# Ternary feed-forward layer: the scaling of the 1408-wide hidden row moves from VectorE to ScalarE

## The reference

```python
def activation_quant(x):
    scale = 127.0 / jnp.clip(jnp.max(jnp.abs(x), axis=-1, keepdims=True), 1e-05, None)
    return jnp.clip(jnp.round(x * scale), -128, 127) / scale

def weight_quant(w):                       # weights of -1, 0, 1
    scale = 1.0 / jnp.clip(jnp.mean(jnp.abs(w)), 1e-05, None)
    return jnp.clip(jnp.round(w * scale), -1, 1) / scale

def bitlinear(x, w):
    return jnp.einsum('bsh,oh->bso', activation_quant(x), weight_quant(w))
...
x = rmsnorm(x, weight)
gate, up = split(bitlinear(x, w_gate_up))  # 512 -> 2 x 1408
hidden = square(relu(gate)) * up
return bitlinear(hidden, w_down)           # 1408 -> 512
```

## Time and profile before

| | |
|---|---|
| median of three runs | 1764.09 us (1761.99, 1764.09, 1770.47) |
| the profiled execution, its own time | 1760.03 us |
| its span, first to last instruction | 1758.3 us |
| busy: PE, DVE, ACT, POOL | 1363.1, 1424.3, 936.0, 545.6 us |
| mean granted TensorE clock | 0.892 of full speed |
| phase L0f | from 224 to 401 us of the span; its matmuls from 233 us |
| L1101, the operation that the change moves | 16 times, 15.3 us in all, 953 ns each |
| L1030, GpSimd's rounding that follows it | 16 times, 45.2 us in all, 2825 ns each |

### The profile page before, as it was taken

The page is one execution under the profiler, slowest core; times in us unless marked ns, Lnnn a source line. Parts: engine busy times, 40 slices in busy tenths (PEclk is TensorE's granted clock), DMA queues, the critical chain, the costliest instruction groups (busy, mean ns, idle before and its releaser), DMA issues. The chain is left out here.

```text
span 1758.3 us, 23962 instructions
## 1 busy us (share of the span) xinstructions
PE 1363.1 (78%) x6614; PEld 1011.7 (58%) x6614; DVE 1424.3 (81%) x3156; ACT 936.0 (53%) x1936; POOL 545.6 (31%) x569
## 2 busy tenths in 40 slices
PE   4889358886999667266771992489999899998888
PEld 2444224444788443254620882368888788876776
DVE  5999769985887468799488799888999889878785
ACT  3477646652333362466425441358888788733443
POOL 0000014442110022200013122214777577766541
PEclk8899779998999757688885996799999999999999
DMA  6230020000000210355200100416889799887974
GB/s 213 90 123 13 0 78 1 0 0 1 1 1 1 86 61 1 93 194 179 68 1 0 48 25 1 125 49 208 248 245 251 210 263 256 251 235 234 261 231 157
DMA packets 92286, 197.93 MB, mean 113 GB/s; under 512 B 16040, under 2 KB 25384, under 8 KB 91312
## 3 DMA queue, kind: packets, MB, share of 16 engines
q0 software_dynamic: 27120, 91.25, 18.9%
q1 hardware_dynamic: 65088, 105.82, 18.3%
HBM read 181.30 MB, written 15.73 MB: 112 GB/s over the span
## 5 line engine op out<-in xcount | busy, mean ns | idle before, releaser
L2379 POOL DMA_INDIRECT L3f_gd<-rows,idx x160 | 188.4, 1178 | 202.2 <-DVE L3f_gd L2608 177.0
L2379 POOL DMA_INDIRECT L3f_gu<-in_L_ffn_e_up,idx x160 | 168.4, 1052 | 71.2 <-issue 47.2
L2447 PE MATMUL L3f_o_ps<-L3f_euh,L3f_ath 128*128 128x512 f32 x352 | 146.4, 416 | 22.4 <-DVE L3f_atl L2589 19.5
L2435 PE MATMUL L3f_h_ps<-L3f_xh,L3f_edh 128*128 128x512 f32 (+1 forms) x384 | 144.0, 375 | 6.7 <-DVE L3f_xl L2594 6.7
L2419 PE MATMUL L3f_g_ps<-L3f_oh 128*128 128x128 f32 x704 | 97.0, 282 | 61.5 <-DVE L3f_oh L2576 61.5
L2435 PE MATMUL L3f_h_ps<-L3f_xh,L3f_edl 128*128 128x512 f32 (+1 forms) x384 | 144.0, 375 | 0.0
L2435 PE MATMUL L3f_h_ps<-L3f_xl,L3f_edh 128*128 128x512 f32 (+1 forms) x384 | 143.9, 375 | 0.0
L1030 POOL TENSOR_TENSOR wgu<-L0f_hid,magic 128x1408 bf16<-128x1408 f32 x16 | 45.2, 2825 | 315.2 <-DVE L0f_hid L1101 315.2
L2447 PE MATMUL L3f_o_ps<-L3f_eul,L3f_ath 128*128 128x512 f32 x352 | 138.9, 395 | 0.0
L2447 PE MATMUL L3f_o_ps<-L3f_euh,L3f_atl 128*128 128x512 f32 x352 | 138.9, 395 | 0.0
L2419 PEld LDWEIGHTS L3f_g_ps<-L3f_oh 128*128 128x128 f32 x704 | 90.9, 194 | 72.0 <-issue 67.4
(11 more groups left out here) (555 smaller groups left out, 3729.3 us busy)
## 6 DMA issues: line engine op xcount, KB each, us to landing
L3f_eu<-in_L_ffn_e_up SPq DMA_DIRECT2D x96, 256.0 KB
L3f_ed<-in_L_ffn_e_down SPq DMA_DIRECT2D x96, 256.0 KB
L2x_ed<-in_L_ffn_e_down SPq DMA_DIRECT2D x32, 256.0 KB, 3.3
rows<-L2x_eo SPq DMA_DIRECT2D x32, 256.0 KB, 2.4
wgu<-in_L_ffn_w_gate_upT SPq DMA_DIRECT2D x4, 1408.0 KB, 7.5
X<-in_x SPq DMA_DIRECT2D x4, 1024.0 KB, 10.2
L0x_V<-in_ctxT SPq DMA_DIRECT2D x8, 512.0 KB, 3.9
L1f_C<-in_ctx SPq DMA_DIRECT2D x2, 2048.0 KB, 12.9
```

The source lines that it names most:

```text
L2379: pool.indirect_dma_start(buf[j % ND][:, :], None, table, bass.IndirectOffsetOnAxis(ap=idx[:, j:j + 1], axis=0)).then_inc(sem[j % ND], 16)
L2435: last = pe.matmul(h_ps[h][:, 0:cols], lhsT=w[h][:, c, :], rhs=x[:, c, 0:cols], start=(c == 0 and m == 0), stop=(c == DC - 1 and m == 2))
L2447: last = pe.matmul(o_ps[a][:, :], lhsT=w[h][:, a * P:(a + 1) * P], rhs=x[h][:, :], start=False, stop=False)
```

## The change

The scaling of the hidden row becomes a ScalarE operation (Identity with scale and bias, where the bias is a column that holds MAGIC). It is issued at the head of ScalarE's turn n for tile n+1, with a wait for that tile's scale; for tile 0 it is issued ahead of the turns, after the first chunk of tile 1. VectorE's L1101 and its wait are removed. GpSimd waits on the same semaphore as before, which ScalarE now raises.

```diff
     @block.scalar
...
-        count_from_two(act, xq_ready, xqT_ready, rl_ready, sq_ready, hqT_ready)
+        count_from_two(act, xq_ready, xqT_ready, rl_ready, sq_ready, hqT_ready, hk_ready)
...
+        def scale_hidden(n, h):
+            act.wait_ge(hs_ready, n + 3)
+            act.activation(hid[h][:, :], hid[h][:, :], ACT.Identity, scale=s[:, bass.ds(n, 1), 6], bias=magic[:, 0:1]).then_inc(hk_ready, 1)
+
         def one(n, h):
+            if within(n, 1):
+                scale_hidden(n + 1, 1 - h)
             hidden_turned(n, h)
...
         for j in range(NCH):
             up(1, 1, j)
+            if j == 0:
+                scale_hidden(0, 0)
         steps(act, one)
...
     @block.vector
...
             dve.tensor_scalar(at(s, n, 6), at(s, n, 6), 127.0, at(s, n, 4), ALU.mult, ALU.mult).then_inc(hs_ready, 1)
-            dve.wait_ge(hs_ready, n + 3)
-            dve.tensor_scalar(hid[h][:, :], hid[h][:, :], at(s, n, 6), MAGIC, ALU.mult, ALU.add).then_inc(hk_ready, 1)
```

More of the change, by code:

```diff
@@ L1038, in _ @@
     def _(dve):
-        count_from_two(dve, xn_ready, am_ready, ac_ready, ar_ready, as_ready, xm_ready, hid_ready, hm_ready, hc_ready, hr_ready, hs_ready, hk_ready, x_ready, st_ready)
+        count_from_two(dve, xn_ready, am_ready, ac_ready, ar_ready, as_ready, xm_ready, hid_ready, hm_ready, hc_ready, hr_ready, hs_ready, x_ready, st_ready)
         n = row_stats(dve, stats, m[:, :], var[:, :], w1[:, :], w2[:, :], step, 0)
```

## The result

| | before | changed |
|---|---|---|
| median of the runs | 1763.04 us (1755.72 to 1770.47, 4 runs) | 1791.09 us (1788.48 to 1794.19, 4 runs) |
| ratio, 95% interval | | 1.0158 (1.0123 to 1.0192) |
| span of the profiled execution | 1758.3 us | 1786.8 us |
| VectorE busy, ScalarE busy | 1424.3, 936.0 us | 1413.2, 955.9 us |
| phase L0f, its first VectorE operation (L100) to the next phase's (L129) | 177.3 us | 205.0 us |

The change costs 28 us, 1.6%. VectorE has 11 us less to do and the kernel is slower by 28: all of it lies in the phase L0f (27.7 us). What comes before the phase ended 1.8 us later in this execution and what comes after it took 1.0 us less, which makes the 28.5 of the spans.

A forecast was written before the change was run, and what follows sets the result against it. VectorE was taken to set the pace in L0f. Ring 25.2, start 0.3, end 1.2 and clock 3.3 make 30.0 us on the profiled 1760.03, so 1790; the median, 3 higher, is 1793 us, range 1782 to 1803.

The forecast's parts named there:

- The ring: L0f loop: chain from scale through scaling, copies, ReLU, square to first product takes 4.2 us, not 2.40; 25.2 us in all.
- hand-over: Signal from VectorE's scale operation to ScalarE's scaling, taken as 0.15 us within the 4.2, bounded by 0.03 and 0.16.
- VectorE's cover: Removing L1101 saves VectorE 0.95 us a turn; alone a turn could gain only 0.41, and here it returns as waiting.
- not slower: Rival: the scaling fits into ScalarE's wait at the turn's head; gain 5.7 us, giving 1757; chance 0.04.
- The start: Tile 0's scaling between the first and second chunk of tile 1 delays products: +0.3 us, between 0 and 0.9.
- The end: Tile 14's down projection waits for copies behind tile 15's scaling: +1.2 us, between 0 and 1.3.
- The clock: TensorE's longer idle before the third chunk halves its clock: 0.7 us in a third of the turns, 3.3 us.
- GpSimd: Its rounding gets its tile about 0.8 us later but has a whole turn of slack; costs nothing.

The follow-up runs named there:

- e5: The changed kernel with 24 extra 128x128 transposes on TensorE ahead of the third chunk; ratio 1.0142 to the kernel before, stage 202.9 us.
- e1: The kernel before with only the wait for the scale put at the head of ScalarE's turn, scaling still on VectorE; ratio 1.0021 to the kernel before.
- e2: The changed kernel with the scaling issued behind ScalarE's two copies of the hidden row instead of ahead; ratio 1.0060 to the kernel before.
- e6: The changed kernel with one more 128x512 f32 ScalarE operation between the wait for the scale and the scaling; ratio 1.0221 to the kernel before.
- e4: The kernel before without any scaling of the hidden row, GpSimd waiting for the scale instead; ratio 1.0025, loop turns 9.31 and 11.22 us.
- e11: The changed kernel run again unaltered; ratio 1.0143 to the kernel before, stage 205.2 us.
- e8: The changed kernel with scaling behind the first chunk's square, split: 704 columns on ScalarE, 704 on VectorE; ratio 1.0129 to the kernel before.
- e3: The changed kernel with the scaling issued behind the first chunk's square; ratio 1.0000 to the kernel before, loop turn 9.67 us.
- e7: The kernel before without scaling of the hidden row, GpSimd's rounding also waiting for VectorE's L1065 of that turn; ratio 0.9961 to the kernel before.
- e9: e8 with GpSimd's rounding also waiting for VectorE's scaling of a token row (L1089); ratio 0.9970 to the kernel before.

## Why the prediction was right

The forecast was 1793 us, 30 us of cost; measured 1791.09, 28 us of cost.

- **The ring (1.8 us a turn, 25.2 in all).** Measured 4.20 us from the scale to the product, forecast 4.2; 7.37 for the rest, forecast 7.3. The 14 turns grew by 26.1 us with the clock's falls and by 25.1 in e5, without them. The hand-over that I bounded by 0.03 and 0.16 was 0.17 (0.04 in e1's turn above, with the copy behind the wait), the scaling 1.56 (forecast 1.55). e1, e2 and e6 move the term as the ring says: the wait alone 0.3 a turn, behind the copies 0.85, with 0.72 us of work more about 0.7 more.
- **VectorE's cover.** I gave the removal of L1101 no gain in the sum, and none is there. Its worth by itself, forecast 0.41 a turn, was 0.38 in e4's short turns. The rival "not slower" fell with L1107's place: ScalarE's wait for it is 46.6 us.
- **The start (+0.3)** did not show: the part until tile 1 took 30.1 us against 30.6.
- **The end (+1.2)** was 2.0. The down projection starts 3.16 us after the start of the last scale's operation instead of 2.00, so the 1.2 itself is right, but the projection then ran longer than before: 4.22 us before, now 4.88 from 419.79 to 424.67. The part after the turns has 6.8 us at the low clock, 3.4 before and in e5, where it took 13.7 us, 0.9 above before.

```profile
416.63 0.21 DVE L1107 TENSOR_SCALAR L0f_s<-L0f_s 128x1 f32<-128x1 f32 x1
419.79 1.89 PE L949 MATMUL L0f_o_ps<-wgu,L0f_hqT 128*128 128x512 bf16 x4 [4.15 <-ACT L0f_hqT L999]
421.90 2.77 PE L949 MATMUL L0f_o_ps<-wgu,L0f_hqT 128*128 128x512 bf16 x6 [0.22 <-issue]
```

- **The clock (3.3 us)** is the mis-sized term. I had a third of the turns hit; six of 14 have a stretch at 0.50. But they cost 1.1 us in all and not 0.7 each: against e5's turns one cost 0.76, two 0.2 and 0.1, three nothing. I took 0.7 from the one turn in which the clock was low from the first matmul of the third chunk; the kernel before has that turn too, so that some of the 1.1 is no growth. In the turn shown above TensorE resumes at full clock (307.79, 0.82 us) and falls only afterwards, by these stretches of the changed kernel:

```profile
308.00:310.00 2.00, 1.48 (x9) 0.59 (x8) 1.96 (x6) 0.96 (x3) 0.88 (x1) 0.74 0.00 0
310.00:312.00 2.00, 2.00 (x8) 0.98 (x9) 1.83 (x4) 1.30 (x3) 0.00 (x0) 0.50 0.00 0
```

The third product is then 3.89 us after the first, hardly late (3.82 before), and what is slow is the down projection, which has slack: that turn is 11.57 us, as the others. The falls in the turns of the changed kernel, e11 and e6 line up by the distance from the first product to the fall, which I had left out (14th turn, which has less work, not counted; by the clock granted in the trace):

| the clock falls, us after the first product | the third product is late by |
|---|---|
| 0.1 to 0.8 (5 falls) | 0.7 to 0.8 |
| 0.9 (3) | 0.55 to 0.57 |
| 1.1 to 1.2 (3) | 0.34 to 0.37 |
| 1.3 and 1.4 (2) | 0.18, 0.11 |
| 1.5 and more (6) | nothing |

So 0.7 is what a fall costs that comes with the third chunk's first matmul, and most come later. Why a fall comes where it does in a turn stays open.

- **GpSimd** I costed at nothing, and that is nearly so by the order of this change and not by slack, as e4 and e8 show. Its rounding starts at 304.73, after VectorE's front operation is over. Its last weight operation meets VectorE's scaling of a token row (L1087 here), which takes 0.66 us in the loop and up to 0.82 instead of 0.49:

```profile
307.88 1.00 POOL L1042 TENSOR_TENSOR Wl<-Wr,Wh  x1 [0.17 <-POOL Wh L1040]
308.50 0.66 DVE L1087 TENSOR_SCALAR L0f_xn<-L0f_xn,L0f_s 128x512 f32<-128x512 f32 x1
```

Of these 0.17 us a loop turn shows under 0.1 (7.37 against 7.3), because the third product has no longer to wait for its square.

The errors (3.3 for about 1, 1.2 for 2.0, 0.3 for none, the ring a little short) went both ways and left 2 us; that the sum is nearer than its terms is luck.

## What to carry to other kernels

An operation moved to a less busy engine is paid in full if it stands between a late signal and the work that the busy engine waits for next; read when its input is made, not how idle the other engine is, and draw the ring with start-to-start times. The same operation cost 28, 10.5 or 0 us by its place in ScalarE's list, and a split of it gained 5. When work is shifted, look also at which GpSimd and VectorE operations now meet, and order them with a wait if need be.

## What the runs showed of the hardware that I had not expected

GpSimd's 128x1408 addition in SBUF and some operations of VectorE exclude each other; the second waits for the first to end. A VectorE operation on two SBUF tensors (L1065, 0.75 us) took 2.88 us when it started 0.20 us after GpSimd's (e4), one of f32 with a scalar (L1089, 0.49 us) 2.34 and 2.21 when it started 0.47 and 0.60 us after it (e8); with L1065 first, GpSimd's took 2.89 instead of 2.53. The last is already in the kernel before: L1030 has 2.89 us there, and 2.53 in the change, where the two don't meet. Other operations of VectorE do not meet it: the products and the output, which read PSUM, ran beside GpSimd's operation in e3 at their usual 0.69 to 0.75 us, and the maximum of a token row (L1067) in the kernel before at 0.69, as always. The Trainium skill, SBUF — State Buffer, SBUF: two separate sides, states this as a lock on a shared pair of ports that whoever starts first holds for the whole instruction, and names the VectorE operations that take it: those with two SBUF inputs and those in a mode with two ports. The traces agree on who waits, with VectorE's end 0.28 us after GpSimd's in e8 and 0.55 in e4; in which mode L1089 runs, none shows. GpSimd's short weight operations do it too: in e2 L1087 (321.75, 0.79 us) ends 0.29 us after one that ran from 321.75 to 322.25. The cost was 1.9 us in a turn of e4, more than the whole scaling on either engine, and 3.4 in one of e8 (12.8 against e9's 9.4). A wait of GpSimd on VectorE's operation took it away (e7 for L1065, e9 for L1089). No wait view shows it: it stands in the duration of the operation.
